# Taking out the identity products that nobody reads, in the first attention and in both gated FFNs

## The reference, cut to what matters

```
x = x + 0.5 * L0_ffn(layernorm(x))     # 16 experts, top 4, and a shared FFN
x = x + L0_attn(layernorm(x))          # causal, state and action of rank 32, one head
x = x + 0.5 * L0_ffn(layernorm(x))
x = x + 0.5 * L1_ffn(layernorm(x))     # gated, 704 wide: silu(g) * u, then down
x = x + L1_attn(layernorm(x))          # 16 heads of 128, rope
x = x + 0.5 * L1_ffn(layernorm(x))
```

## Time and profile before

| what | value |
|---|---|
| median of 3 runs (lowest, highest) | 2043.96 us (2040.21, 2044.92) |
| the profiled execution's own time | 2039.38 us |
| its span | 2037.6 us |
| its mean granted TensorE clock | 0.997 |
| instructions | 40489 |
| PE busy | 1951.3 us, 96% |
| DVE, ACT, POOL busy | 70%, 65%, 46% |

### The profile page before, as it was taken

How to read it: one execution, slowest core, us unless ns; L and a number is a source line. 1 busy time by engine, 2 the same in 40 slices (tenths; PEclk the granted TensorE clock), 3 DMA queues, 4 the chain that set the end, 5 groups by cost and what they waited for, 6 DMA issues and landing times. The chain is left out here.

```text
span 2037.6 us, 40489 instructions
## 1 busy us (share of the span) xinstructions
PE 1951.3 (96%) x13831; PEld 1766.5 (87%) x13831; DVE 1423.7 (70%) x3588; ACT 1317.5 (65%) x3368; POOL 947.1 (46%) x974
## 2 busy tenths in 40 slices
PE   6988989898999999999999999999999999999899
PEld 4767867687899999999999999999999999998788
DVE  8348763545868777786877778787777878777653
ACT  4335633444778687777867777787777778777652
POOL 1642116534455536454553645545365454636242
PEclk9999999999999999999999999999999999999999
DMA  7752057700000000000000000000000000000010
GB/s 251 215 83 32 33 166 211 156 10 9 9 6 9 9 6 4 7 9 9 6 9 6 4 6 9 9 7 9 6 4 7 9 9 7 9 6 1 2 47 32
DMA packets 58602, 73.46 MB, mean 36 GB/s; under 512 B 9760, under 2 KB 45216, under 8 KB 58272
## 3 DMA queue, kind: packets, MB, share of 16 engines
q1 hardware_dynamic: 43808, 53.83, 8.2%
q0 software_dynamic: 14592, 17.04, 5.0%
HBM read 51.06 MB, written 19.80 MB: 35 GB/s over the span
## 5 line engine op out<-in xcount | busy, mean ns | idle before, releaser
L1184 ACT ACTIVATE phase_p<-phase_scores,phase_bias 128x512 f32<-128x512 f32 (+3 forms) x680 | 417.5, 628 | 117.0 <-DVE phase_bias L1172 116.3
L1230 DVE TENSOR_TENSOR phase_pt_lo<-phase_ring,phase_pt_hi 128x512 fp32r<-128x512 f32 (+3 forms) x680 | 390.3, 603 | 89.6 <-ACT phase_pt_hi L1225 85.8
L1225 ACT ACTIVATE phase_pt_hi<-phase_ring 128x512 fp32r<-128x512 f32 (+3 forms) x680 | 342.9, 536 | 106.2 <-PE phase_ring L1210 102.1
L1210 PE MATMUL phase_ring<-sb_ident,phase_p 128*128 128x128 f32 x2312 | 340.8, 274 | 10.8 <-ACT phase_p L1184 4.5
L160 PE MATMUL phase_y<-phase_pt_hi,phase_v_hi 128*128 128x256 f32 (+1 forms) x1152 | 341.5, 296 | 6.6 <-DVE phase_y_lo L2293 6.6
L161 PE MATMUL phase_y<-phase_pt_lo,phase_v_hi 128*128 128x256 f32 (+1 forms) x1152 | 321.5, 279 | 0.0
L162 PE MATMUL phase_y<-phase_pt_hi,phase_v_lo 128*128 128x256 f32 (+1 forms) x1152 | 321.4, 279 | 0.0
L1210 PEld LDWEIGHTS phase_ring<-sb_ident,phase_p 128*128 128x128 f32 x2312 | 272.2, 141 | 51.0 <-ACT phase_p L1184 14.0
L1165 DVE TENSOR_REDUCE phase_peaks<-phase_scores 128x1 f32<-128x512 f32 (+1 forms) x408 | 265.6, 665 | 46.3 <-PE phase_scores L1152 43.8
L2316 POOL TENSOR_TENSOR phase_straight<-phase_rot,late_rope 64x512 f32<-64x512 f32 x128 | 163.7, 1279 | 274.4 <-ACT phase_rot L2188 274.3
L2333 POOL TENSOR_TENSOR sb_x<-sb_x,phase_part 128x512 f32<-128x512 f32 x128 | 164.8, 1288 | 253.5 <-ACT phase_part L2223 247.1
(11 more groups left out here) (272 smaller groups left out, 4857.4 us busy)
## 6 DMA issues: line engine op xcount, KB each, us to landing
phase_e_up<-expert_up SPq DMA_DIRECT2D x32, 352.0 KB, 4.8
phase_e_dn<-expert_down SPq DMA_DIRECT2D x32, 256.0 KB, 5.4
y_rows<-phase_zero SPq DMA_DIRECT2D x16, 512.0 KB, 7.7
sb_x<-y_rows POOLq DMA_DIRECT2D x16, 512.0 KB, 6.6
xn_rows<-phase_ln_xn SPq DMA_DIRECT2D x8, 512.0 KB, 2.9
late_raw_qk<-qk SPq DMA_DIRECT2D x16, 256.0 KB, 2.6
sb_x<-x SPq DMA_DIRECT2D x4, 512.0 KB, 5.7
phase_raw_up<-up SPq DMA_DIRECT2D x8, 256.0 KB, 4.5
```

Source lines behind the costliest of these rows:

```text
L1184: act.activation(self.p[:, at:at + width], self.scores[:, at:at + width], ACT.Exp, bias=self.bias[:, t % 2:t % 2 + 1], accum_out=self.sums ...
L1210: done = pe.transpose(bank[:, j * P:(j + 1) * P], self.p[:, (4 * place + j) * P:(4 * place + j + 1) * P], self.core.ident[:])
L1225: act.activation(hi, value, ACT.Copy).then_inc(*self.t_hi.one)
L1230: dve.tensor_tensor(lo, value, as_f32(hi), ALU.subtract).then_inc(*self.t_lo.one)
```

## The change

The method `keep_warm`, the table `IDLE` and all calls are taken out. Nothing else moves; the constant `ident_b` is still loaded, and the result is computed by the same products in the same order.

```diff
-    def keep_warm(self, pe, bank, count):
-
-        for _ in range(count):
-            pe.matmul(bank.rearrange("p (a b) -> p a b", b=P), self.ident_b[:], self.ident_b[:].unsqueeze(1).broadcast_to([P, BANK // P, P]),
-                      start=True, stop=True)
...
-    IDLE = {("flip", 0, 0): 22, ("state", 0): 6, ("score", 0, 0, 0): 9, ("score", 0, 1, 0): 5}
...
         for step in self.order:
             what = step[0]
-            if step in self.IDLE:
-                core.keep_warm(pe, self.y[:], self.IDLE[step])
...
     def pe(self, pe):
-        bank = self.down_ps[:, 0, :]
-        if 0 in self.ahead:
-            self.core.keep_warm(pe, bank, 6)
-        else:
-            self.core.keep_warm(pe, bank, 20)
+        if 0 not in self.ahead:
             self.pe_turn(pe, 0, 0)
-            self.core.keep_warm(pe, bank, 5)
         for c in range(NCH):
```

## The result

| | before | after |
|---|---|---|
| median of 20 runs each | 2041.37 us | 2045.64 us |
| lowest, highest | 2038.39, 2047.73 | 2041.93, 2052.93 |
| ratio after to before, 95% interval | | 1.0020 (1.0013 to 1.0026) |
| span of the profiled execution | 2037.6 us | 2043.1 us |
| mean granted TensorE clock | 0.997 | 0.987 |

The account below looks back on a forecast made before the run. TensorE, busy 96% of the span, was taken to bound the kernel. Attention 2.2, gated0 0.3 and gated1 0.2 sum to 2.7 us, on the median 2043.96 giving 2046.7 us; range 2041.5 to 2052.5.

Parts of the forecast that it names:

- case A: The forecast itself: two or three short cold starts, the one in attention paid; -1 to +4.1 us; chance 0.44.
- Hidden work: Attention and gated FFNs: most removed products stand before waits; gain taken as 0 in attention, up to 0.2 us in gated1.
- rival D: Attention: the 5 products at 147.94 stand on the path; 2.3 us come back with gated1's 0.2 (2041.7); chance 0.07.
- Attention: First attention's start: cold transposes 0.6 us plus eight cold state and action products 1.6; 2.2 us, between 0 and 3.0.
- The clock was back after 3.2 to 3.4 us: Attention's state and action: recovery time read from the stretches; 3.4 us makes 8 products cold, 1.6 us.
- if it falls again there, that is nothing new: Attention, 145 to 150 us, where the values are made: the low clock there costs little as it is.
- rival B: Attention: clock may not settle before the second state and action; 7.0 us, up to 1.3 more in gated0; chance 0.38.
- the sign that the prediction named for B: Attention: a clock of 0.50 in the second state and action, still 0.50 at about 157 us.
- The transposes: Attention's start: by the skill's rule eight transposes leave the clock low, 2.2 us; by the trace they may raise it, 0.6.
- rival C: Attention and gated0: transposes raise the clock by themselves; 0.6 us and a little is left (2044.6); chance 0.11.
- Gated0 and gated1: Gated FFN starts: waits cover gated0's 2.2 us, 0.3 taken (0 to 1.3); gated1 0.2 (-0.2 to 1.0).

Follow-up runs that it names:

- the narrow products: The attention's 42 identity products kept in number and place but with 128 columns each instead of 512, against the kernel before: ratio 1.0014, +2.9 us (1.0 to 4.9).

## Why the prediction was right or wrong

**The number: in part luck.** The 2046.7 us are 2043.96, a median of three runs, plus 2.7. The median of 20 runs of before is 2041.37, and the same sum on it gives 2044.1, 1.6 us less than the 2045.64 that were measured. The base was too high, and the cost too low, and the two nearly cancelled.

**Sign and cause: right.** The kernel is slower by 4.1 us where 2.7 were forecast, inside the range and at the edge of what the forecast case A held (up to 4.1). The cost is the clock's: the narrow products show it, the rows of cold transposes and products, and the granted clock of all runs (0.982 to 0.988 against 0.991 to 0.997).

**Hidden work: right.** The 22, 6, 9, 20 and 5 were taken as hidden; nothing moved sooner for their removal but the flips of chunk 1, by 0.3 us of the 2.11 at stake. So rival D fell.

**Attention: mis-sized.** The term was 0.6 + 1.6 = 2.2 us, between 0 and 3.0. It measured 2.5 at the first score in the profile after (0.4 at the first state product, for the 0.6, and 2.2 behind it, for the 1.6), and 4.0 over the attention. With the attention alone changed it was 2.2 at the first score and 2.8 over the attention in the profile, and 3.3 (1.2 to 5.3) over the runs. Two things in the working failed. "The clock was back after 3.2 to 3.4 us" was read from stretches in which TensorE had work at once. Here eight transposes and a pause came first, and from the first product it took 4.7 us (138.31 to about 143), ten products and not eight. And "if it falls again there, that is nothing new" was wrong: it did fall again at 146, but stayed low to about 160 instead of 150, and took eight products of the second state and action with it, 1.4 us. That is rival B's mechanism, and the sign that the prediction named for B (a clock of 0.50 in the second state and action, and at about 157 us) is there in the profile after. The price is not: 1.4 of the 4.0 us that B charged beyond the first chunk, as B had taken all twelve as cold, and the flips and the values as paid. In the other profile of the same attention code, with the attention alone changed, the second state was warm. So A's cause is what happened, with a part of B's in some executions. That the fall at 146 costs next to nothing when it ends by 150 does hold: of the four profiles with this code as before, two have no fall there, and the attention lasts 130.16 and 130.90 us in them, 130.46 and 131.81 in the two that have it.

**The transposes.** Eight of them at 134.53 did not bring the clock up; it was 0.50 still at 138.31 and up to about 143. So rival C fell. That is as the Trainium skill ("TensorE: Matmul & The Clock Gate", Part 4) would have it, where transposes do not count as busy in the same way. It does not single the transposes out, though, since of ordinary products too it took ten here. And the sixteen of the earlier trace rows did bring it up, so the rule as it stands there does not hold for all transposes in this kernel. (PEclk reads 1.00 over the first 17 us; that those sixteen were cold is seen by their pace of 0.23 us.) With only the 22 out, the eight cold transposes and the six identity products behind them (135.93 to 139.71) were followed by warm state products, where after, without the six, ten state products were cold.

**Gated0 and gated1: right.** 0.3 and 0.2 were forecast; the two together measured 0.8 (-1.0 to 2.7). The fourth piece of gated0 did not move (14.03 against 14.05 us), as forecast, though ten products were cold; 0.4 us came behind it, at the turning of chunk 1. The 0.54 of gated1 are the transfer's in this pair of profiles.

**Chances.** Within 0.2% had 0.55 and slower 0.38. The ratio of 1.0020 stands on that bound, and neither is borne out over the other.

## What to carry to other kernels

Filler products are free only in front of a wait, and only if they end before it does: 17 placed where TensorE had work cost 3.5 us, and five that ran cold held up the next product by 1.2. In front of a wait they can be worth more than they look: the price of a low clock is paid in the dense work behind the stall, so count the products that follow it on the path and the idle time that covers them. Here eight transposes ahead of a pause of 1.84 us did not bring the clock back, and once it was back the stalls of 2.21 and 2.08 us took it away again. Measure such a change in many runs, and compare a stage over all profiles whose code is the same there: routed1, which nobody touched, lasts from 112.05 to 116.70 us in fourteen profiles.

## What the runs showed of the hardware that was not expected

Forty-two products of 128 columns did no good that could be measured: +2.9 us (1.0 to 4.9) against the kernel with as many of 512 at the same places, and +3.3 (1.2 to 5.3) with none. A cold stretch could last far beyond the stall that began it: from about 133 to 143 and from 146 to 160 us after, against 3.4 us at the longest in the earlier trace rows. The same code in routed1 had its clock fall near 270 us in eight of the twelve experiments' profiles and in that of after, and not in the others; routed1 was on average 2.2 us longer with it. The runs of one kernel lie up to 11.0 us apart (after, 2041.93 to 2052.93; before, 9.3), and in each kernel the longer runs tend to be those with the lower granted clock (correlation -0.49 to -0.96). So falls at different places are one cause of this spread; what share of it they make up was not measured.
